# Gated delta rule: the two Gram matrices together, the sigmoid of the decays in quarters, state scalings moved between chunks

## The reference, cut to what matters

```python
q = silu(dwconv(x @ Wq));  k = silu(dwconv(x @ Wk));  v = silu(dwconv(x @ Wv))
a = sigmoid(x @ Wa + ba);  beta = sigmoid(x @ Wb + bb)
def step(S, t):                       # S: (b, h, 128, 128), a[..] per value row
    y = einsum('bhvk,bhk->bhv', S, k_t);  err = y - v_t
    S = a_t[..., None] * S - (b_t[..., None] * err)[..., None] * k_t[:, :, None, :]
    o = einsum('bhvk,bhk->bhv', S, q_t)
o = layernorm(o) * sigmoid(x @ Wg);  return o @ Wo
```

## Time and profile before

| | us |
|---|---|
| median of 3 runs | 2659.15 |
| profiled execution | 2658.91 |
| its span | 2657.0 |
| clock of PE granted, mean | 0.852 |
| this layer, from the first slot's heads to the last slot's norm | about 1040 to 2330 |

### The profile page before, as it was taken

How to read it: one execution, slowest core, us unless ns; L and a number is a source line. 1 busy time by engine, 2 the same in 40 slices (tenths; PEclk the granted TensorE clock), 3 DMA queues, 4 the chain that set the end, 5 groups by cost and what they waited for, 6 DMA issues and landing times. The chain is left out here.

```text
span 2657.0 us, 45220 instructions
## 1 busy us (share of the span) xinstructions
PE 2083.4 (78%) x16876; PEld 1611.6 (61%) x16888; DVE 1521.6 (57%) x3266; ACT 1182.6 (45%) x2893; POOL 1037.5 (39%) x965
## 2 busy tenths in 40 slices
PE   8497438978897987857798577977779676768798
PEld 5365225646565865746587466866668665546586
DVE  2222642237574344687676876767868678246532
ACT  3212411126364334754465545655456454326433
POOL 0222122210003552586335862467724757100254
PEclk9698769989998997958798687986689777889899
DMA  8422012110004212321222212322122222020430
GB/s 281 134 24 53 3 43 67 23 44 2 23 2 134 102 18 75 97 69 49 84 90 68 89 45 83 93 69 69 57 88 80 66 69 78 19 58 2 118 118 16
DMA packets 138317, 179.47 MB, mean 68 GB/s; under 512 B 62048, under 2 KB 114544, under 8 KB 132992
## 3 DMA queue, kind: packets, MB, share of 16 engines
q1 hardware_dynamic: 129952, 166.46, 20.5%
q0 software_dynamic: 8160, 10.26, 2.5%
HBM read 154.52 MB, written 22.17 MB: 66 GB/s over the span
## 5 line engine op out<-in xcount | busy, mean ns | idle before, releaser
L2672 DVE SCALAR_TENSOR_TENSOR XT<-M_delta,CW_delta,XT 128x256 f32<-128x256 f32 x576 | 250.0, 495 | 82.7 <-ACT M_delta L2463 52.6
L2146 PE MATMUL PS<-XP_delta,X 128*128 128x268 f32 (+1 forms) x1024 | 244.0, 391 | 15.5 <-DMA X<-in_L_attn_b_heads 15.5
L2146 PEld LDWEIGHTS PS<-XP_delta,X 128*128 128x128 f32 x1024 | 194.8, 191 | 68.2 <-DMA X<-in_L_attn_b_heads 19.3
L1541 PE MATMUL PS<-XP_rffn,UW_rffn 128*128 128x512 f32 x816 | 195.3, 396 | 5.1 <-POOL UW_rffn L1495 4.6
L1541 PEld LDWEIGHTS PS<-XP_rffn,UW_rffn 128*128 128x128 f32 x816 | 156.4, 192 | 38.9 <-issue 6.0
L1273 ACT ACTIVATE PR_attn<-PS,NM_attn 128x256 f32<-128x256 f32 (+1 forms) x384 | 131.0, 449 | 102.5 <-DVE NM_attn L1343 102.5
L1495 POOL TENSOR_TENSOR UW_rffn<-W_rffn,UW_rffn 128x512 fp32r<-128x512 f32 x34 | 43.7, 1286 | 298.8 <-ACT UW_rffn L1602 298.8
L561 POOL DMA_INDIRECT sums<-XS_moe,token_moe x46 | 71.7, 1559 | 220.8 <-ACT XS_moe L661 196.9
L2590 ACT ACTIVATE S_delta<-S_delta,AO_delta 128x128 f32<-128x128 f32 x512 | 156.9, 396 | 0.0
L1663 DVE TENSOR_TENSOR SU_rffn<-PS,CB_rffn 128x512 f32<-128x512 f32 x68 | 47.0, 692 | 179.7 <-PE PS L1541 157.3
L1504 POOL TENSOR_TENSOR HP_rffn<-HF_rffn,HP_rffn 128x512 fp32r<-128x512 f32 x68 | 92.5, 1380 | 116.3 <-ACT HP_rffn L1625 116.3
(11 more groups left out here) (459 smaller groups left out, 5271.4 us busy)
## 6 DMA issues: line engine op xcount, KB each, us to landing
M_delta<-gram_delta SPq DMA_DIRECT2D x32, 1280.0 KB, 5.9
X<-in_L_attn_b_heads SPq DMA_DIRECT2D x64, 512.0 KB, 3.5
EW<-in_L_ffn_w SPq DMA_DIRECT2D x24, 512.0 KB, 9.1
CB_rffn<-routes_rffn SPq DMA_DIRECT2D x20, 512.0 KB, 21.9
XN<-in_L_attn_b_outs SPq DMA_DIRECT2D x16, 512.0 KB, 3.6
F_delta<-in_L_attn_b_outs SPq DMA_DIRECT2D x4, 2048.0 KB, 9.5
W_rffn<-in_L_ffn_tiles SPq DMA_DIRECT2D x4, 1536.0 KB, 12.5
slots<-pad SPq DMA_DIRECT2D x2, 2967.0 KB, 14.3
```

The source lines that it names most:

```text
L1541: last = nc.tensor.matmul(PS[:, 4 + 2 * n + q, :], UW[qw][:, r, (q * KD + k) * P:(q * KD + k + 1) * P], XP[qx][:, k, n * NB:(n + 1) * NB], ...
L2146: last = nc.tensor.matmul(PS[:, 1 + i, 0:B * (WIN - halo)], WH[:, r, i, k, :], XP[:, k, :, n * BT + halo:n * BT + WIN], start=(k == 0), st ...
L2672: nc.vector.scalar_tensor_tensor(TMP[:, r, i], RAW[:, r, i, :, tau:tau + BT], CW[:, i, h, tau:tau + 1], TMP[:, r, i], ALU.mult, ALU.add).t ...
```

## The change

Four edits. The heads are cut in two parts, 0 to 13 and 14 to 15, and PE makes both groups' Gram products of the first part, then of the second; `gram(1)` after the states goes, and `gram_rows` on DVE follow in the new order, all four ahead of the state copies. The first scatter waits for three of the four. The sigmoid becomes four instructions of 128x1024, one behind each of the first four steps of the states on ACT. `cuts` become 18, 18, 24 and 4 lanes, and in a group's last chunk the remaining 4 scalings stand ahead of the key rows. The number of arithmetic operations is unchanged but for three more ACT instructions per slot.

```diff
--- before.py
+++ after.py
@@ -1922,7 +1922,7 @@
             def chunks(n):
 
                 z = base_of(n)
-                sp.wait_ge(gr_d, z["gr_d"] + 2)
+                sp.wait_ge(gr_d, z["gr_d"] + 3)
                 scatter(0, 0)
                 sp.wait_ge(conv_d, z["conv_d"] + 3 * H)
                 spread(n, 0)
@@ -2147,9 +2147,9 @@
                                                 XP[:, k, :, n * BT + halo:n * BT + WIN], start=(k == 0), stop=(k == KD - 1))
                     last.then_inc(p_mm, 1)
 
-            def gram(o):
-
-                for h in range(H):
+            def gram(o, first, last_h):
+
+                for h in range(first, last_h):
                     for b in range(B):
                         lane = B * h + b
                         last = nc.tensor.matmul(
@@ -2380,10 +2380,12 @@
                 z = base_of(n)
                 heads_and_norm(n)
                 pe.wait_ge(ev_d, z["ev_d"] + 3 * H)
-                pe.wait_ge(act_d, z["act_d"] + 3 * H)
                 pe.wait_ge(raw_d, z["raw_d"] + H)
-                pe.wait_ge(k_d, z["k_d"] + H)
-                gram(0)
+                for first, last in ((0, H - 2), (H - 2, H)):
+                    pe.wait_ge(act_d, z["act_d"] + 3 * last)
+                    pe.wait_ge(k_d, z["k_d"] + last)
+                    for o in range(NO):
+                        gram(o, first, last)
                 if n:
                     pe.wait_ge(y_d, z["y_d"])
                 for g in range(NS + 1):
@@ -2391,7 +2393,6 @@
                         state_t(n, 0, g)
                     if g >= 1:
                         columns(n, 0, g - 1)
-                gram(1)
                 for o in range(NO):
                     key_products(n, o)
                     cross_products(n, o, range(1))
@@ -2544,6 +2545,11 @@
                         state_copy(n, o, g)
                     if g >= 1:
                         f_copy(n, o, g - 1)
+                    if not o and g < 4:
+                        part = AF[:, g * BH * BT // 4:(g + 1) * BH * BT // 4]
+                        last = nc.scalar.activation(part, part, ACT.Sigmoid)
+                        if g == 3:
+                            last.then_inc(a_d, 1)
                     if 2 <= g < 2 * NI + 1:
                         keys_apart(n, o, g - 2)
 
@@ -2595,12 +2601,11 @@
                 act.wait_ge(nw_mm, base_of(n)["nw_mm"] + HOPS * o + hop_no(jj, s) + 1)
                 nc.scalar.copy(TR[:, 2], PS[:, 6, :]).then_inc(nw_d, 1)
 
-            cuts = [0, 14, 28, 48, BH]
+            cuts = [0, 18, 36, 60, BH]
             for n in range(NBLK):
                 z = base_of(n)
                 heads_and_norm(n)
                 act.wait_ge(raw_d, z["raw_d"] + H)
-                nc.scalar.activation(AF, AF, ACT.Sigmoid).then_inc(a_d, 1)
                 states(n, 0)
                 for o in range(NO):
                     key_products(n, o)
@@ -2629,6 +2634,8 @@
                             act.wait_ge(wdec_d, z["wdec_d"] + rests(o, jj))
                             for x in range(jj):
                                 natural(x)
+                        if jj == NI - 1:
+                            decay_state(lane, last)
                         for r in rows[:2]:
                             key_rows(n, o, r)
                         if gates:
@@ -2639,10 +2646,9 @@
                                 gate(n, h)
                                 lane, then = then, min(then + 3, last)
                                 decay_state(lane, then)
-                        else:
+                        elif jj + 1 < NI:
                             decay_state(lane, last)
-                            if jj + 1 < NI:
-                                answer(n, ci)
+                            answer(n, ci)
                         for r in rows[2:]:
                             key_rows(n, o, r)
                     for r in range(NR):
@@ -2675,7 +2681,7 @@
 
             def gram_rows(n, o, i):
 
-                dve.wait_ge(gr_mm, n * 4 + 2 * o + i + 1)
+                dve.wait_ge(gr_mm, n * 4 + 2 * i + o + 1)
                 beta = NBETA[:, NO * n + o, 8 * i:8 * i + 8]
                 nc.vector.tensor_tensor(GR[:, o, 8 * i:8 * i + 8], PS[:, 1 + 2 * o + i, :].rearrange("p (h w) -> p h w", h=8),
                                         beta.unsqueeze(2).broadcast_to([P, 8, 2 * OC]), ALU.mult).then_inc(gr_d, 1)
@@ -2843,12 +2849,11 @@
             for n in range(NBLK):
                 z = base_of(n)
                 heads_and_norm(n)
-                gram_rows(n, 0, 0)
-                gram_rows(n, 0, 1)
+                for i in range(2):
+                    gram_rows(n, 0, i)
+                    gram_rows(n, 1, i)
                 for g in range(1, NS, 2):
                     state_copy(n, 0, g)
-                gram_rows(n, 1, 0)
-                gram_rows(n, 1, 1)
                 for o in range(NO):
                     if o == 0 and n:
                         dve.wait_ge(y_d, z["y_d"])
```

## The result

The kernel before took 2659.15 us (median of 7 runs on the chip of the comparison), the changed one **2639.36** (median of 7, 2628.3 to 2649.7): ratio **0.9931 [0.9908, 0.9954]**. The forecast was 2637.4.

A forecast was written before the change was run, and what follows sets the result against it. No engine was near full (PE busy 78%); chains passing from engine to engine in three stretches bound the changed layer. Sum: 2658.9 - 6.0 (starts) - 20.7 (group 1 ends) + 4.8 + 0.4 (scalings elsewhere) = 2637.4 us, range 2624 to 2650.

The forecast's parts named there:

- The end of group 1: Group 1's last chunk: key rows 2 and 3 no longer wait behind 16 scalings; 20.7 us gained over four slots.
- Group 0's last chunk: Four scalings delay POOL and lock out L2755: 1.2 us lost per slot, 4.8; the chunk before loses 0.4 in all.
- Gram in the pause: Slot start: first Gram part runs at the full clock while PE waits for key scaling; states start 3.07 us earlier.
- Sigmoid in quarters: Slot start on ACT: load 1.28, four quarters of 1.05 us between state copies; POOL starts 4.0 us later.
- The locks at L2712: First chunk: VectorE and POOL take turns; 1.35 us into POOL's chain, up to 0.7 more for the first base.
- The sum of a start: Slot start to GH's scaling: 1.5 us gained per slot, 6.0 for four; bounds 3.3 and 0.
- states at the low clock: Rival at the slot's start: clock falls to 0.50 and stays, 17.7 us more per slot, 2708; chance 0.06.
- The drain: Rival at ACT's table load: some 1.38 us of drain added to each load, about 2643; chance 0.05.

The follow-up runs named there:

- e_group0: Changed kernel with group 0 of each slot back on the old cuts 14, 14, 20, 16, group 1 on the new: 2632.48 us, ratio 0.9928.
- e_start: Changed kernel with the old cuts and the old place of the scalings, so only the slot-start edits: 2651.48 us, ratio 0.9983.
- e_half: Changed kernel with only gram(0) in the pause and gram(1) left behind the states: 2642.33 us, one run.
- e_gram: Kernel before with only both Grams in the pause, old cuts and the sigmoid whole: 2655.98 us, ratio 0.9999.
- e_ends: Kernel before with only the new cuts and the scalings moved: 2641.38 us, ratio 0.9938.
- e_warm: Changed kernel with 7 filler transposes on PE behind the second and fourth step of the states: 2646.05 us, ratio 0.9975.
- e_sigmoid: Kernel before with only the sigmoid in quarters, the Grams where they were: 2670.98 us, ratio 1.004.
- again2: Changed kernel unaltered, run a third time to see the granted clock in each slot's states: 2637.08 us, one run.
- e_early: Changed kernel with the table load and first sigmoid quarter ahead of the first state copy: 2628.48 us, ratio 0.9906.
- e_best: Changed kernel with group 0's old cuts, and table load and first sigmoid quarter ahead of the first state copy: 2618.9 us, ratio 0.9866.

## Why the prediction was right, and where not

- **The end of group 1 (20.7).** Right in mechanism, 19.1 in size. Counted from group 1's L2041, the turn comes 5.55, 2.55, 4.68 and 4.49 us earlier than before, against the 4.4 forecast, and the update (in the last slot the norm) 5.39, 4.16, 4.40 and 5.18, against 5.1, 5.2, 5.1 and 5.3. PE still waits 1.40 us for ACT's key rows (4.23 us for all sixteen instructions of the four rows). In the second slot DVE's queries decided, as said; in the first and third, where the turn ran at the low clock, 1.05 and 0.80 us of idle time remain. The prediction had named the clock at the turn as what decides this.
- **Group 0's last chunk (-4.8, -0.4).** Right: L2761 took 2.86 in every slot instead of 1.70, the step to the turn is 1.16, 1.28, 1.08 and 1.10 longer, 4.6 in all (both terms, 5.2, lie in this step), and in the trace of `e_group0` it is gone. The 1.6 us between this turn and the update were in no term: the prediction asked for the clock at the turn of group 1 only. PE's wait before group 0's turn grew from between 1.0 and 1.6 us to between 2.2 and 2.4, and the turn then ran wholly or partly at 0.50 in three of the four slots.
- **Gram in the pause (3.07 per slot earlier).** The step that failed is "7/8 of two Grams at 2.01 is 3.5 us, until 1419.2": the instructions run at that pace, but PE stopped for 1.1 to 1.5 us between two of them, waiting for its next block of instructions, which no term had, and the last two heads stood behind it. The states start 1.97 earlier after the raw decays, not 3.07.
- **Sigmoid in quarters.** Its parts were right: 1.28 for the load, 1.06 to 1.09 a quarter (1.05 forecast). `a_d` came 13.7 after the raw decays instead of 12.7, as the states it is threaded through came 1.1 later.
- **The locks at L2712.** Right: POOL's chain from L2062 to the end of L2036 took 19.7 instead of 18.1, so 1.6 were lost (1.12 at L2019 beside L2718, 0.45 at L2036 beside the first `base`), within the 1.35 to 2.05 forecast. The Trainium skill (SBUF — State Buffer, section on the two separate sides) says that an instruction of VectorE with two SBUF inputs and one of GpSimd that reads SBUF exclude each other; here 2.06 against 1.47 and 1.73 against 0.61, and L2761 with 2.86 against 1.70, agree.
- **The sum of a start.** POOL starts 4.98 later (forecast 4.0), loses 1.6 to the locks and had 7.34 idle: 0.7 gained, measured 0.72. With the forecast's 4.0 it is 1.7. So the miss of 1 us per slot is the stop. A start gains 0.8 and not 1.5, as `e_start` shows. That the stop accounts for it is a sum; `e_half`, which has no stop, starts POOL 1.25 us earlier, but is bound elsewhere.
- **The rival "states at the low clock"** (0.06) was real in part: in two of the three traces of the changed kernel it takes one slot for 13.7 us and costs 3.5 to 4.3 there, not 17.7; in the third it lasts 3.4 us. The forecast let the clock stay down for the whole stretch of 21.8. In the trace of `e_gram`, where PE waited in one piece, it came in every slot.
- **The drain** did not occur: the first quarter starts 0.01 us after the load's 1.28 (1420.55 to 1421.84), on the path to `a_d`. The Trainium skill (ScalarE: Activation LUTs, What ACT_TABLE_LOAD costs) gives 1.38 us of drain; this trace does not show it.

With the measured sizes the sum is 2658.9 - 3.3 + 4.6 + 1.6 - 19.1 = 2642.7, without a fall of the clock in the states; the median is 2639.4, the forecast 2637.4. The terms missed by 2.7 us at the starts, 1.6 at the ends and 1.6 at group 0's turn, all to the same side, and by 0.6 to the other at the locks. So that the median lies only 2.0 from the forecast is in part luck, while the large term, nine tenths of the gain with `e_ends` alone, was right in mechanism.

Left open: why the clock falls in the states of one execution and not in those of another with the same load. The load of this stretch does not decide it: in the fourth slot of `e_warm` PE was busy for only 5.5 of the first 8 us of states and the clock stayed at 1.00, while in slots of the changed kernel with 6.5 it fell in some executions.

## What to carry to other kernels

When you move work out of an engine's last step before a hand-over, move it only in the group where that step is the one waited for: the same edit gained 19 us at group 1 and lost 6 at group 0, through a lock between two other engines and the low clock that followed on a third. When a long instruction is cut up to let small ones in between, put the first piece into the idle time ahead of the first small one. Two edits that depend on each other (`e_gram` 0, `e_sigmoid` -11, together +3) must be priced as one. Before a dense run of very short instructions is moved into a pause, price the supply of instructions to that engine: here it took back a third of what the move gave (1.1 of 3.07 us).

## What the runs showed of the hardware

- **PE waits for its instructions in dense runs of short multiplications.** With 128x32 weights and 64 columns, one every 16 ns, PE stood still for 1.1 to 1.9 us in the changed kernel and its variants with "issue" as the only reason, after 142, 158 and 174 instructions in the slots 1 to 3, the same in each execution (in `e_warm`, whose program is longer, after 128, 130 and 132), and after 126 in slot 0 in all but `again2`. Second stops come 127 multiplications after the first (2.17 us in `e_warm`, 0.3 to 0.9 in slot 0). All 43 end 1.20 to 1.53 us after a 16 KB packet of the queue "q8 instruction" has come in. It happened once with a multiplication every 26 ns too (`e_sigmoid`, first slot, 0.61 us). In the kernel before, the 128 of `gram(1)` ran without a stop at the same pace (2.01 us); there the last packet had come in 0.4 us or more before they began.
- **The clock.** After an idle stretch of 2.21 to 2.95 us in the states PE ran at 0.50 (1.2 GHz) for 6.8 to 10.2 us in every slot of `e_gram`. After a wait of 2.17 to 2.77 us before group 0's turn, the turn ran wholly or partly at 0.50 in 27 of 28 slots; after one of 1.01 to 1.61, in 3 of 24. With several gaps of about 1 us (busy 2.77 of 4 us) it fell in some executions only. In the eight slots of `e_early` and `e_best`, with PE busy for 7.4 us or more of the first 8 us of states, it stayed at 1.00.
- **The lock.** L2761, a VectorE instruction with two SBUF inputs, takes 0.41 us with POOL idle and 1.70 or 2.86 beside POOL's L2099; in both cases it ends 0.28 to 0.29 us after L2099 does.
